# Projection ahead of attention: first sums by tile, transfers and maxima moved

## The chip, the cores and the metric

The kernel runs on one core of a Trainium2 chip. The metric is the device time of one execution in microseconds, the median of several. PE is the tensor engine (PEld its weight loads), DVE the vector engine, ACT the scalar engine, POOL GpSimd, SP the engine that here only issues transfers.

## The reference, cut to what matters

A block of a transformer on 2 x 2048 tokens of 512 channels: a mixture of experts, attention, the mixture of experts again, each behind a layer norm without scale or bias:

```
x = x + 0.5 * ffn(layernorm(x));  x = x + attn(layernorm(x));  x = x + 0.5 * ffn(layernorm(x))
attn: q = x @ Wq + bq  (16 heads of 32)    k = x @ Wk + bk, v = x @ Wv + bv  (one head of 32)
      out = softmax(q k^T / sqrt(32)) v @ Wo + bo
```

The change lies in the projection, which makes q, k and v of `layernorm(x)` and stores `x + bo`.

## The kernel before, in words

Stages follow each other with a barrier between them: `route` and `experts`, then `project` and the rest of `attention`, then `route`, `experts` and `combine`. Each engine runs its own instructions in the order in which they are written, and waits at semaphores (`wait_ge`). The order is written out by hand; there is no planner.

`project` (from line 1094) takes the 4096 tokens as 32 tiles of 128, and four tiles as a turn (`TURN`, eight turns, `NTURN`). The experts left x in two tensors in memory that have to be added. For turns 0 and 1 (`ADDED`) both are loaded (`got`, `other`, line 1184 and 1186) and DVE adds them tile by tile (`add_sums`, 1366). For the later turns SP loads one, and POOL issues a transfer that adds the second to it (`bring`, 1242), which waits for the load first. Four turns are loaded at once (`LEAD`), the others as the loop of SP comes to them. `got` has six buffers.

The work on tile t is spread over slots, and in slot s every engine does what is due of several tiles:

- DVE `moments` of tile s-1 (1374 to 1381: mean and variance), after `add_sums` of tile s in the first eight slots;
- POOL `deviation` of tile s-1 (1228, 1231: one over the square root, and the shift), after `output_bias` of tile s-4 (1237: adds `bo` to x);
- ACT `normalise` of tile s-2 (1324) and `high` of tile s-3 (1331: the part of the transposed tile that goes to PE in reduced precision);
- PE `transposes` of tile s-3 (1263), DVE `low` of tile s-4 (1388: the rest);
- PE `keys` (K and V, twelve matmuls, lines 1268 to 1270) at the first slot of a turn from slot 8 on, `queries` (twelve matmuls for one of four groups of heads) in every slot from 8 to 39, and `values` (1288, small transposes) in the third slot of a turn;
- one slot later ACT and DVE take the results: `queries` (ACT 1336 the high part `qhi`, DVE 1394 the low part `qlo`), `keys` (ACT 1342 to 1347, DVE 1400), `values` (DVE 1404). SP stores both parts of a query (`store_q`, 1195 and 1197), and ACT overwrites a part only when the store of a turn ago has landed (`s_q`).

In the last 16 slots (`FIRST` = 24) the stage also does 64 blocks of row maxima of scores ahead for the first group of attention (`first_maxima`): PE makes a block of 128 x 512 scores in one of two banks of PSUM, `pF` (1298), and DVE reduces it (1408). PE waits until the reduction of two blocks earlier is done. Each of these slots has four (`SOME`): two ahead of all other work of the slot, two behind it, on PE and on DVE. Their queries are read back from memory by SP after turn 3 (`ahead["queries"]`, 12 transfers, line 1452).

`FIRST`, `SOME` and the slot offsets stand at the top of the function; `SLOTS` is 41. `first_blocks(s, half)` gives the block numbers of half a slot.

Of the kernel before, what the change touches and what calls it, by code (L numbers as in the profile page):

```python
# [23 lines left out]
TURN = 4  # L24
# [11 lines left out]
A = 32  # L36


def begin(eng, *sems):
    for s in sems:  # L40
        eng.sem_inc(s, A)  # L41
# [1052 lines left out]
def project(nc, tag, k, prep, q_d, kT, v_sb, sums, xb_d, ahead):  # L1094
# [17 lines left out]
    with ExitStack() as ctx:  # L1112
# [16 lines left out]
        pV = m.ps("pV", [P, TURN, DH])  # L1129
        pF = m.ps("pF", [P, 2, 512])  # L1130
        s_g = m.sems("g", RING)
        s_on = m.sems("on", RING)
        s_xo = m.sems("xo", RING)
        s_add = m.sem("add")
# [23 lines left out]

        def loads(i):

            return i // RING + (2 if i % RING < ADDED else 1)

        def brought(i):
            return i // RING + (0 if i % RING < ADDED else 1)

        def first_blocks(s, half):

            n = SOME * (s - FIRST) + SOME // 2 * half
            return range(n, n + SOME // 2) if 0 <= n < ahead["items"] else ()

        def comes(t):
            return 0 <= t < NT
# [4 lines left out]
        with nc.Block() as block:  # L1177
            @block.sync
            def _(sp):
                begin(sp, *s_q, *s_g, *s_xo)  # L1180

                def load(i):
                    sp.wait_ge(s_xo[i % RING], A + i // RING * 16)
                    sp.dma_start(got[i % RING][:, :, :], turn_view[0][i, :, :, :]).then_inc(s_g[i % RING], 16)
                    if i < ADDED:
                        sp.dma_start(other[i][:, :, :], turn_view[1][i, :, :, :]).then_inc(s_g[i % RING], 16)

                def store_x(i):
                    sp.wait_ge(s_xb, A + (i + 1) * TURN)
                    dst = xb_d[i * (TURN * P):(i + 1) * (TURN * P), :].rearrange("(t p) c -> p t c", p=P)  # L1190
                    sp.dma_start(dst, got[i % RING][:, :, :]).then_inc(s_xo[i % RING], 16)

                def store_q(c, g):
                    sp.wait_ge(s_hi, A + c * GPC + (g + 1))
                    sp.dma_start(q_view[c, g, 0, :, :], qhi[g].bitcast(F32)).then_inc(s_q[g], 16)
                    sp.wait_ge(s_lo, A + c * GPC + (g + 1))
                    sp.dma_start(q_view[c, g, 1, :, :], qlo[g].bitcast(F32)).then_inc(s_q[g], 16)

                for i in range(LEAD):
                    load(i)  # L1200
                for i in range(NTURN + 1):
                    if i + LEAD < NTURN:
                        load(i + LEAD)
                    for g in range(GPC):

                        if g == 2 and i < NTURN:
                            store_x(i)
                        if i > 0:
                            store_q(i - 1, g)
                    if i == 3:  # L1210
                        for g in range(GPC):
                            sp.wait_ge(s_q[g], A + 32)
                        ahead["queries"](sp)
                for b in range(RING):
                    sp.wait_ge(s_xo[b], A + 16 * len(range(b, NTURN, RING)))
                for g in range(GPC):
                    sp.wait_ge(s_q[g], A + 32 * CHUNKS)

            @block.gpsimd
            def _(pool):  # L1220
                begin(pool, s_rd, s_rs, s_xb)

                def deviation(t, j):
                    pool.wait_ge(s_ve, A + t + 1)
                    pool.sem_inc(k["pool_on"], 1)
                    pool.wait_ge(s_xn, A + t - TURN + 1)
                    pool.sem_inc(k["pool_on"], 1)
                    pool.tensor_tensor(rstd[:, j:j + 1], ve[:, j:j + 1], k["half"][:, 0:1], ALU.pow).then_inc(s_rd, 1)
                    pool.wait_ge(s_rd, A + t + 1)
                    pool.sem_inc(k["pool_on"], 1)  # L1230
                    pool.tensor_scalar(shift[:, j:j + 1], mv[:, j, 0:1], rstd[:, j:j + 1], -1.0, ALU.mult, ALU.mult
                                       ).then_inc(s_rs, 1)

                def output_bias(t):
                    pool.wait_ge(s_xn, A + t + 1)
                    pool.sem_inc(k["pool_on"], 1)
                    pool.tensor_tensor(x_tile(t), x_tile(t), bo_sb[:, :], ALU.add).then_inc(s_xb, 1)

                def bring(i):
                    pool.wait_ge(s_g[i % RING], A + 16 * loads(i))  # L1240
                    pool.sem_inc(k["pool_on"], 1)
                    pool.dma_start(got[i % RING][:, :, :], turn_view[1][i, :, :, :], accum_op=ALU.add
                                   ).then_inc(s_on[i % RING], 16)

                for s in range(SLOTS):

                    i = (s + 6) // TURN
                    if (s + 6) % TURN == 0 and ADDED <= i < NTURN:
                        bring(i)
                    if comes(s - BIAS):  # L1250
                        output_bias(s - BIAS)
                    if comes(s - 1):
                        deviation(s - 1, (s - 1) % TURN)

            @block.tensor
            def _(pe):
# [6 lines left out]
                        ins = pe.transpose(pT[:, j % 2, c, :], xn[:, j, c * P:(c + 1) * P], k["ident"][:, :])  # L1263
                    ins.then_inc(s_tr, 1)

                def products(out, high, low, b):
                    for c in range(CK):
                        pe.matmul(out, high[:, c, :], xh[b][:, c, :], start=c == 0, stop=False)
                        pe.matmul(out, high[:, c, :], xl[b][:, c, :], start=False, stop=False)
                        ins = pe.matmul(out, low[:, c, :], xh[b][:, c, :], start=False, stop=c == CK - 1)  # L1270
                    return ins

                def queries(i, g, b):
                    pe.wait_ge(s_lo, A + i * GPC + (g - 1))
                    own = slice(g * P, (g + 1) * P)
                    products(pQ[:, g % 2, :], wqh[:, :, own], wql[:, :, own], b).then_inc(s_pq, 1)

                def keys(i, b):
                    pe.wait_ge(s_xl, A + (i + 1) * TURN)
# [11 lines left out]
                def first_maxima(n):  # L1291
                    unit, part = n // (S // 512), n % (S // 512)
                    t, h = unit // HG, unit % HG
                    if n == 0:
                        pe.wait_ge(ahead["in"], A + 48)
                        pe.wait_ge(s_kl, A + CHUNKS // 2)
                    pe.wait_ge(ahead["reduced"], A + n - 1)
                    pe.matmul(pF[:, n % 2, :], ahead["q"][0:3 * DH, h, t * P:(t + 1) * P],
                              kT[0:3 * DH, part * 512:(part + 1) * 512], start=True, stop=True
                              ).then_inc(ahead["made"], 1)  # L1300

                for s in range(SLOTS):
                    for n in first_blocks(s, 0):
                        first_maxima(n)
                    if comes(s - TRANS):
                        transposes(s - TRANS, (s - TRANS) % TURN)
                    if comes(s - PROD):
                        i, j = (s - PROD) // TURN, (s - PROD) % TURN
                        if j == 0:
                            keys(i, i % 2)  # L1310
                        queries(i, j, i % 2)
                        if j == 2:
                            values(i)
                    for n in first_blocks(s, 1):
                        first_maxima(n)

            @block.scalar
            def _(act):
# [42 lines left out]
            def _(dve):  # L1361
                begin(dve, s_add, s_st, s_ve, s_vb, s_xl, s_lo, s_kl, ahead["reduced"])

                def add_sums(t, i, j):
                    dve.wait_ge(s_g[i % RING], A + 16 * loads(i))
                    dve.tensor_tensor(x_tile(t), x_tile(t), other[i][:, j, :], ALU.add).then_inc(s_add, 1)

                def moments(t, i, j):
# [39 lines left out]
                    dve.tensor_reduce(ahead["mx"][:, n:n + 1], pF[:, n % 2, :], X, ALU.max).then_inc(ahead["reduced"], 1)  # L1408

                for s in range(SLOTS):  # L1410
                    for n in first_blocks(s, 0):
                        first_maxima(n)
                    if comes(s - SPLIT):
                        low(s - SPLIT, (s - SPLIT) // TURN, (s - SPLIT) % TURN)
                    if s < ADDED * TURN:
                        add_sums(s, s // TURN, s % TURN)
                    if comes(s - 1):
                        moments(s - 1, (s - 1) // TURN, (s - 1) % TURN)
                    if comes(s - PARTS):
                        i, j = (s - PARTS) // TURN, (s - PARTS) % TURN  # L1420
                        queries(i, j)
                        if j == 1:
                            keys(i)
                        if j == 3:
                            values(i)
                    for n in first_blocks(s, 1):
                        first_maxima(n)
                dve.wait_ge(ahead["reduced"], A + ahead["items"])
                dve.wait_ge(s_kl, A + NTURN)
# [650 lines left out]
```

## Time and profile before

| | us |
|---|---|
| median of 3 runs without a profile | 3122.11 (3119.02 to 3122.38) |
| the profiled execution, own time | 3151.85 |
| its span, first to last instruction | 3150.1 |
| projection, from its first transfer to the next stage's first work on DVE | 616.6 to 816.4 |
| PE busy in the whole span | 2751.5 (87%) |
| DVE, POOL, ACT busy | 2045.3, 2243.3, 1523.3 |

The page gives busy time per engine. A busy share of PE is no distance from the end: what counts is which engine the others wait for in a stretch. The views used below are the stretches (busy time of each engine between two times), the waits (who waited for whom) and the timeline (instructions in order of time). The mean granted clock of PE is 0.931 of full speed over the span; it is 0.50 from 616 to 650 us and 1.00 from 660 to 816.

### The profile page before, as it was taken

The page shows a single profiled execution, that of the slowest core. Times are in us where ns is not written, and L with a number is a line of the kernel's source. Part 1 is how long each engine was busy: PE and PEld are TensorE (multiplying, and loading weights), DVE is VectorE, ACT ScalarE, POOL GpSimd, SP SyncE. Part 2 cuts the span into 40 slices and gives each one's busy share as a digit, 9 for nine tenths or more (in the row PEclk, how much of TensorE's full clock was granted, in tenths as well). Part 3 has the DMA queues.
Part 4 walks back from the last instruction along what each step waited for, and adds up shares of the span by engine and source line. Part 5 has one row for each costly group of instructions (what it writes and reads, how often), then busy time and mean ns, then how long its engine had stood idle before and what let it go on. Part 6 is the DMA issues. An engine that isn't in the chain of part 4 may idle for free. (4 is left out here: it accounts for less than half of the span.)

```text
span 3150.1 us, 44567 instructions
## 1 busy us (share of the span) xinstructions
PE 2751.5 (87%) x15016; PEld 1648.4 (52%) x15016; DVE 2045.3 (65%) x3954; ACT 1523.3 (48%) x2871; POOL 2243.3 (71%) x1461
## 2 busy tenths in 40 slices
PE   7967777489899999999999999999999776888870
PEld 4644444266555555555555555555554474555540
DVE  7843222257788888788788887887874494333334
ACT  5622222153476666566566665765656451222220
POOL 2248888563399979799798897997989323778770
PEclk9979888689999999999999999999999767999995
DMA  5579999895388888799797887987877454999998
GB/s 209 212 208 247 236 237 240 182 287 193 84 183 180 170 179 177 153 194 181 165 184 159 188 166 157 194 173 174 175 149 165 139 211 136 221 234 241 234 183 325
DMA packets 221450, 608.27 MB, mean 193 GB/s; under 512 B 34476, under 2 KB 35500, under 8 KB 193320
## 3 DMA queue, kind: packets, MB, share of 16 engines
q0 software_dynamic: 91760, 376.49, 59.2%
q1 hardware_dynamic: 125240, 220.55, 21.3%
q10 hardware_dynamic: 4224, 8.39, 0.7%
q8 instruction: 121, 1.98, 0.3%
q14 instruction: 105, 0.86, 0.1%
HBM read 230.94 MB, written 155.24 MB: 123 GB/s over the span
## 5 line engine op out<-in xcount | busy, mean ns | idle before, releaser
L1924 DVE TENSOR_REDUCE attention_mx<-attention_pM 128x1 f32<-128x512 f32 x1984 | 1209.3, 682 | 185.1 <-PE attention_pM L1808 184.3
L1755 ACT ACTIVATE attention_prob<-attention_pS 128x512 f32<-128x512 f32 x2048 | 1032.7, 627 | 566.4 <-PE attention_pS L1787 561.7
L1692 POOL TENSOR_TENSOR attention_pair<-attention_prob 128x1024 f32<-128x1024 f32 x380 | 989.8, 2768 | 108.5 <-ACT attention_prob L1755 105.1
L1787 PE MATMUL attention_pS<-attention_qT,prep_kT 128*128 128x512 f32 x2048 | 841.3, 413 | 4.7 <-ACT attention_prob L1755 3.8
L1808 PE MATMUL attention_pM<-prep_kT,attention_qT 96*128 96x512 f32 x1984 | 787.8, 398 | 0.8
L1787 PEld LDWEIGHTS attention_pS<-attention_qT,prep_kT 128*128 128x128 f32 x2048 | 387.3, 189 | 313.0 <-issue 210.2
L768 POOL DMA_INDIRECT sum<-experts_res,c_table x256 | 403.5, 1576 | 124.3 <-issue 82.3
L1836 PE MATMUL attention_pO<-attention_prob,attention_v 128*32 128x512 f32 x4096 | 491.7, 598 | 0.0
L1808 PEld LDWEIGHTS attention_pM<-prep_kT,attention_qT 96*128 96x128 f32 x1984 | 377.9, 190 | 89.3 <-DVE attention_mx L1924 14.4
L752 POOL DMA_INDIRECT experts_rows<-xn_rows,c_table x256 | 250.1, 977 | 104.1 <-issue 74.9
L797 PE MATMUL experts_pT<-c_ident,experts_rows 128*128 128x128 f32 x1024 | 169.8, 307 | 117.1 <-issue 68.0
L943 DVE TENSOR_SCALAR experts_res<-experts_pD,experts_rows 128x512 f32<-128x512 f32 x128 | 93.5, 749 | 271.0 <-DMA sum<-experts_res,c_table 170.4
L1836 PEld LDWEIGHTS attention_pO<-attention_prob,attention_v 128*32 128x32 f32 x4096 | 110.1, 109 | 252.7 <-issue 147.6
L1692 POOL TENSOR_TENSOR prep_acc<-attention_prob 128x1024 f32<-128x1024 f32 x68 | 167.0, 2493 | 86.6 <-ACT attention_prob L1755 83.7
L797 PEld LDWEIGHTS experts_pT<-c_ident,experts_rows 128*128 128x128 f32 x1024 | 141.5, 209 | 152.5 <-issue 121.6
L922 DVE COPY experts_xT<-experts_pT 128x512 f32<-128x512 f32 x128 | 88.3, 690 | 204.5 <-PE experts_pT L797 143.7
L892 ACT ACTIVATE experts_res<-experts_pD,experts_rows 128x512 f32<-128x512 f32 x128 | 85.3, 686 | 250.4 <-DMA sum<-experts_res,c_table 180.0
L309 POOL TENSOR_TENSOR route_eqp<-route_eq,route_count 128x1536 f32<-128x1536 bf16 (+1 forms) x16 | 48.4, 3024 | 201.9 <-ACT route_count L429 201.9
L1692 POOL TENSOR_TENSOR attention_acc<-attention_prob 128x1024 f32<-128x1024 f32 x64 | 158.8, 2541 | 5.6 <-ACT attention_prob L1755 2.2
L884 ACT ACTIVATE experts_sg<-experts_pU 128x256 f32<-128x256 f32 x80 | 30.7, 383 | 265.6 <-PE experts_pU L814 121.2
L878 ACT ACTIVATE experts_xT<-experts_pT 128x512 f32<-128x512 f32 x128 | 76.4, 597 | 115.1 <-PE experts_pT L797 59.4
L814 PE MATMUL experts_pU<-experts_xT,experts_wup 128*64 128x256 f32 x1024 | 126.1, 402 | 1.6 <-DVE experts_xT L922 1.6
(184 smaller groups left out, 3195.3 us busy)
## 6 DMA issues: line engine op xcount, KB each, us to landing
prep_acc<-attention_pair POOLq DMA_DIRECT2D x96, 1024.0 KB, 8.1
attention_acc<-attention_pair POOLq DMA_DIRECT2D x90, 1024.0 KB, 7.7
attention_qT<-q_parts SPq DMA_DIRECT2D x96, 256.0 KB
xn_rows<-route_xn SPq DMA_DIRECT2D x16, 1152.0 KB, 6.6
experts_wup<-in_L_ffn_w_up_dram SPq DMA_DIRECT2D x64, 256.0 KB
q_parts<-prep_acc SPq DMA_DIRECT2D x64, 256.0 KB, 4.3
prep_acc<-prep_acc POOLq DMA_DIRECT2D x16, 1024.0 KB, 7.5
ahead_wup<-in_L_ffn_w_up_dram SPq DMA_DIRECT2D x64, 256.0 KB, 9.1
```

What stands on the lines that cost most here:

```text
L752: pool.indirect_dma_start(rows[e % RING][:, a * HALVES + h, :], None, xn_d, bass.IndirectOffsetOnAxis(ap=k["table"][:, 2 * e + a, h:h + 1] ...
L768: pool.indirect_dma_start(sums[a], bass.IndirectOffsetOnAxis(ap=k["table"][:, 2 * e + a, h:h + 1], axis=0), res[e % 2][:, a, h, :], None, ...
L797: t = pe.transpose(pT[:, half, o:o + P], rows[e % RING][:, a * HALVES + h, c:C:CK], k["ident"][:, :])
L814: t = pe.matmul(pU[n % 2][a * H:(a + 1) * H, v, :], wts[b][0][:, a, c, v * H:(v + 1) * H], xT[e % 2][:, c, a, :], start=c == 0, stop=c == ...
L922: dve.tensor_copy(xT[e % 2][:, 2:4, a, :], pT[:, 1, :].rearrange("p (c n) -> p c n", c=2)).then_inc(s_cd, 1)
L943: dve.tensor_scalar(res[e % 2][:, 1, h, :], pD[:, h, 1, :], rows[e % RING][:, HALVES + h, C + 2 * e + 1:C + 2 * e + 2], None, ALU.mult).th ...
L1692: pool.tensor_tensor(to[:, part], prob[2 * n % PROBS][:, part], prob[(2 * n + 1) % PROBS][:, part], ALU.add).then_inc(s_pair, 1)
L1755: act.activation(prob[t % PROBS][:, h * QT:(h + 1) * QT], pS[:, at, :], ACT.Exp).then_inc(s_ex, 1)
L1787: pe.matmul(pS[:, n % 3, :], kT[:, key:key + P], qT[g][:, h, :], start=True, stop=True).then_inc(s_sc, 1)
L1808: pe.matmul(pM[:, r % RING, :], qT[g][0:3 * DH, h, t * P:(t + 1) * P], kT[0:3 * DH, key:key + 512], start=True, stop=True).then_inc(s_mp, 1)
L1836: ins = pe.matmul(pO[h * DH:(h + 1) * DH, :], v_sb[:, batch * STEPS + t, :], prob[t % PROBS][:, h * QT:(h + 1) * QT], start=t == 0, stop=t ...
L1924: dve.tensor_reduce(mx[:, unit, part:part + 1], pM[:, r % RING, :], X, ALU.max).then_inc(s_mr, 1)
```

## The change

Five edits, all in `project`:

1. The first turn is loaded tile by tile: eight transfers (two tensors, four tiles) in the place of two, each pair with a semaphore of its own (`s_first`), for which `add_sums` waits in turn 0.
2. `bring(i)` is issued in slot 4i - 4 in the place of 4i - 6.
3. POOL does `deviation` ahead of `output_bias`.
4. DVE does `moments` of the tile before ahead of `add_sums`.
5. The four maxima of a slot stand on PE among the products of that slot's query, one ahead of each three matmuls, and on DVE all four behind the slot's other work.

```
-            return i // RING + (2 if i % RING < ADDED else 1)
+            return i // RING + (2 if 0 < i % RING < ADDED else 1 if i % RING else 0)      # loads(i)
...
-        def first_blocks(s, half):
-            n = SOME * (s - FIRST) + SOME // 2 * half
-            return range(n, n + SOME // 2) if 0 <= n < ahead["items"] else ()
+        def first_blocks(s):
+            n = SOME * (s - FIRST)
+            return tuple(range(n, n + SOME)) if 0 <= n < ahead["items"] else ()
...
SP
-                for i in range(LEAD):
+                for j in range(TURN):
+                    for part, to in ((0, got[0]), (1, other[0])):
+                        sp.dma_start(to[:, j, :], turn_view[part][0, :, j, :]).then_inc(s_first[j], 16)
+                for i in range(1, LEAD):
                     load(i)
...
POOL
-                    i = (s + 6) // TURN
-                    if (s + 6) % TURN == 0 and ADDED <= i < NTURN:
+                    i = (s + 4) // TURN
+                    if (s + 4) % TURN == 0 and ADDED <= i < NTURN:
                         bring(i)
+                    if comes(s - 1):
+                        deviation(s - 1, (s - 1) % TURN)
                     if comes(s - BIAS):
                         output_bias(s - BIAS)
-                    if comes(s - 1):
-                        deviation(s - 1, (s - 1) % TURN)
...
PE
-                def products(out, high, low, b):
+                def products(out, high, low, b, blocks=()):
                     for c in range(CK):
+                        if blocks:
+                            first_maxima(blocks[c])
...
                 for s in range(SLOTS):
-                    for n in first_blocks(s, 0):
-                        first_maxima(n)
...
-                        queries(i, j, i % 2)
+                        queries(i, j, i % 2, first_blocks(s))
...
-                    for n in first_blocks(s, 1):
-                        first_maxima(n)
...
DVE
                 def add_sums(t, i, j):
-                    dve.wait_ge(s_g[i % RING], A + 16 * loads(i))
+                    if i == 0:
+                        dve.wait_ge(s_first[j], A + 32)
+                    else:
+                        dve.wait_ge(s_g[i % RING], A + 16 * loads(i))
...
                 for s in range(SLOTS):
-                    for n in first_blocks(s, 0):
-                        first_maxima(n)
                     if comes(s - SPLIT):
                         low(s - SPLIT, (s - SPLIT) // TURN, (s - SPLIT) % TURN)
+                    if comes(s - 1):
+                        moments(s - 1, (s - 1) // TURN, (s - 1) % TURN)
                     if s < ADDED * TURN:
                         add_sums(s, s // TURN, s % TURN)
-                    if comes(s - 1):
-                        moments(s - 1, (s - 1) // TURN, (s - 1) % TURN)
...
-                    for n in first_blocks(s, 1):
+                    for n in first_blocks(s):
                         first_maxima(n)
```

## Rows read from the trace of the kernel before

**Rows 1.** Stretches: bounds, length, busy us (count) of five engines, PEclk, DMA share, GB/s
```profile
625.00:630.00 5.00, 0.36 (x2) 0.36 (x3) 4.46 (x11) 0.81 (x1) 1.03 (x2) 0.50 1.05 391
...
680.00:700.00 20.00, 20.00 (x101) 16.20 (x100) 11.06 (x25) 10.94 (x18) 12.21 (x16) 1.00 1.08 314
...
741.00:766.00 25.00, 22.39 (x100) 16.05 (x99) 20.37 (x39) 10.05 (x16) 8.42 (x12) 1.00 0.35 131
```

**Rows 2.** Waits of PE from 616 to 790 us: total, times, longest
```profile
PE attentionp_pF L1298 <- DVE attention_mx L1408: 6.6, 12, 0.6
```

**Rows 3.** Timeline, the head: start, duration, engine, line, operation
```profile
616.62 0.38 SPq L1184 DMA_DIRECT2D attentionp_got<-sum  x1
...
624.47 1.29 DVE L1366 TENSOR_TENSOR attentionp_got<-attentionp_got,attentionp_other 128x512 f32<-128x512 f32 x2 [29.84 <-DMA attentionp_other<-sum]
...
633.17 1.37 POOL L1242 DMA_DIRECT2D attentionp_got<-sum  x1 [4.44 <-DMA attentionp_got<-sum]
...
635.36 0.27 POOL L1231 TENSOR_SCALAR attentionp_shift<-attentionp_mv,attentionp_rstd 128x1 f32<-128x1 f32 x1 [0.21 <-POOL attentionp_rstd L1228]
...
635.66 0.81 ACT L1324 ACTIVATE attentionp_xn<-attentionp_got,attentionp_shift,attentionp_rstd 128x512 f32<-128x512 f32 x1 [6.08 <-POOL attentionp_shift L1231]
...
636.57 1.27 POOL L1237 TENSOR_TENSOR attentionp_got<-attentionp_got,prep_bo 128x512 f32<-128x512 f32 x1
...
636.99 0.69 DVE L1388 TENSOR_TENSOR attentionp_xl<-attentionp_pT,attentionp_xh 128x512 fp32r<-128x512 f32 x1 [6.57 <-ACT attentionp_xh L1331]
...
647.66 0.81 ACT L1324 ACTIVATE attentionp_xn<-attentionp_got,attentionp_shift,attentionp_rstd 128x512 f32<-128x512 f32 x1 [2.69 <-POOL attentionp_shift L1231]
...
649.29 0.78 PE L1268 MATMUL attentionp_pK<-attentionp_xh,prep_wkvh 128*128 128x512 f32 x1
```

**Rows 4.** Timeline, PE: first maxima, products of the keys in two turns
```profile
715.25 0.63 PE L1298 MATMUL attentionp_pF<-prep_kT,attention_qT 96*128 96x512 f32 x2
...
716.87 0.39 PE L1268 MATMUL attentionp_pK<-attentionp_xh,prep_wkvh 128*128 128x512 f32 x1
...
741.67 0.40 PE L1268 MATMUL attentionp_pK<-attentionp_xh,prep_wkvh 128*128 128x512 f32 x1
...
742.37 0.40 PE L1268 MATMUL attentionp_pK<-attentionp_xh,prep_wkvh 128*128 128x512 f32 x1
```

**Rows 5.** Timeline, PE: maxima and transposes around the end of slot 24
```profile
721.77 0.63 PE L1298 MATMUL attentionp_pF<-prep_kT,attention_qT 96*128 96x512 f32 x2
...
722.95 1.10 PE L1298 MATMUL attentionp_pF<-prep_kT,attention_qT 96*128 96x512 f32 x2 [0.55 <-DVE attention_mx L1408]
...
723.88 0.60 PE L1263 MATMUL attentionp_pT<-c_ident,attentionp_xn 128*128 128x128 f32 x4
...
727.12 0.63 PE L1298 MATMUL attentionp_pF<-prep_kT,attention_qT 96*128 96x512 f32 x2
```

**Rows 6.** Timeline, DVE in slots 26 and 27
```profile
732.58 0.68 DVE L1400 TENSOR_TENSOR prep_kT<-attentionp_k,prep_kT 32x512 fp32r<-32x512 f32 x1
...
736.09 0.69 DVE L1388 TENSOR_TENSOR attentionp_xl<-attentionp_pT,attentionp_xh 128x512 fp32r<-128x512 f32 x1
...
737.86 0.75 DVE L1394 SCALAR_TENSOR_TENSOR prep_acc<-attentionp_pQ,prep_bqs,prep_acc 128x512 fp32r<-128x512 f32 x1
...
738.85 2.57 DVE L1408 TENSOR_REDUCE attention_mx<-attentionp_pF 128x1 f32<-128x512 f32 x4 [0.24 <-PE attentionp_pF L1298]
```

**Rows 7.** Timeline, ACT in slot 25
```profile
725.52 0.69 ACT L1336 ACTIVATE prep_acc<-attentionp_pQ,prep_bqs 128x512 fp32r<-128x512 f32 x1 [4.26 <-DMA q_parts<-prep_acc]
```

**Rows 8.** Timeline, the end of the stage
```profile
810.53 0.63 PE L1298 MATMUL attentionp_pF<-prep_kT,attention_qT 96*128 96x512 f32 x2
...
810.97 1.29 DVE L1408 TENSOR_REDUCE attention_mx<-attentionp_pF 128x1 f32<-128x512 f32 x2 [1.56 <-PE attentionp_pF L1298]
...
812.18 0.74 DVE L1394 SCALAR_TENSOR_TENSOR prep_acc<-attentionp_pQ,prep_bqs,prep_acc 128x512 fp32r<-128x512 f32 x1
```

**Rows 9.** The line of the queries' low stores, its last line
```profile
DMA to landing us min/median/max: 2.0/3.3/14.1
```

More of the change, by code:

```diff
@@ L1131, in project @@
         s_g = m.sems("g", RING)
+        s_first = m.sems("first", TURN)
         s_on = m.sems("on", RING)
@@ L1179, in _ @@
             def _(sp):
-                begin(sp, *s_q, *s_g, *s_xo)
+                begin(sp, *s_q, *s_g, *s_first, *s_xo)
                 def load(i):
@@ L1271, in products, with queries @@
                     return ins
-                def queries(i, g, b):
+                def queries(i, g, b, blocks):
                     pe.wait_ge(s_lo, A + i * GPC + (g - 1))
                     own = slice(g * P, (g + 1) * P)
-                    products(pQ[:, g % 2, :], wqh[:, :, own], wql[:, :, own], b).then_inc(s_pq, 1)
+                    products(pQ[:, g % 2, :], wqh[:, :, own], wql[:, :, own], b, blocks).then_inc(s_pq, 1)
                 def keys(i, b):
```

## The prediction, made before the changed kernel ran

> **What bounds the kernel now.** I read the stretches first. All edits lie in `project`, from 616.6 us (its first transfer) to 816.4 us. It has three phases. Until 649.29 PE waits for the first keys. Then PE is busy without a gap: 20.00 of 20.00 us in the second row of [rows 1]. From slot 24 on (715.25, [rows 4]) it is busy 22.39 of 25.00 us, the third row, and the waits say for whom it stops: the next maximum's matmul waits for a reduction of DVE [rows 2]. So PE's order of work is the path in the last two phases, and in the first whatever brings tile 5 to PE, since `keys(0)` stands behind the transposes of tile 5.
>
> **The head now.** I read it next, in order of time. The DMAs bring 391 GB/s [rows 1]; two turns' tensors of 1.05 MB each land for the first sum at 624.47. POOL then stands at `bring(2)` (slot 2) until turn 2's load is there at 633.17: 4.44 us idle, and the deviations of tiles 1 and 2, whose moments were ready, come after it: shift of tile 1 at 635.36 + 0.27 = 635.63. Tile 5 is normalised at 647.66 and the first product of the keys starts at 649.29, so 1.63 us from one to the other [rows 3].
>
> **The change, part by part.** A slot ends, at E, where PE's last matmul of it lets the next one start.
>
> *Transfers two slots later, deviation ahead of the bias.* POOL now has the deviations of tiles 0, 1 and 2 ahead of `bring(2)`, which stands in slot 4 and still waits for 633.17. I take its issue at today's price, so that the shift made behind it is again done at 635.63, but it is tile 3's and not tile 1's. The row at 635.66 (normalise) leads to the low part at 636.99 [rows 3]; in the new order this low part is tile 2's, and tile 5's moments follow it. Low part and moments take 737.86 - 736.09 = 1.77 [rows 6], so they are ready at 638.76. POOL meanwhile does bias 0 (1.27), deviation 4 (0.94, from 635.63 to 636.57), bias 1 and deviation 5: 635.63 + 1.27 + 0.94 + 1.27 + 0.94 = 640.05 [rows 3], later than the moments, so POOL sets it. Plus 1.63 and the sequencers' steps: the keys start at about 641.8. That is 7.5 us sooner. Of these, bias ahead of deviation (the old order) would cost one 1.27 back. Every later `bring(i)` has five slots instead of seven until its turn's moments. Slots before 24 take some 4 us of PE, so some 20 us are left, while the slowest landing in this stage is 14.1 us [rows 9]; no stall there. Bounds for this part: 3 (the wait turns up at tile 3 and costs two more slots) to 9.
>
> *First sums by tile.* Eight transfers of 0.26 MB in the place of two of 1.05 MB. From 616.62 to 624.47 are 7.85 us, of which 2.10 MB at 391 GB/s take 5.4, so 2.5 is latency; the first pair of 0.52 MB should land 2.5 + 1.3 = 3.8 us after the first issue, at about 620.4, four sooner. But these four us are hidden: with the first sum at 624.5 the moments of tile 3 would be ready about 632.7, still before `bring(2)` is through. I take 0 to 0.5 and count nothing. SP has six more issues and four more semaphores to start; an issue takes 0.38 [rows 3], 2.3 us in all, beside transfers that already queue. If they delayed turn 2's load, all of that delay would stand on the path: 0 to 2, I take 0.
>
> The row says that the stream runs at 391 GB/s with transfers of 1 MB. The Trainium skill (DMA: Bandwidth & Descriptors, Anatomy of one DMA, and Bandwidth) counts about 2.0 us fixed per DMA beside its bytes and says to batch to 1 MiB or more. By that, if the fixed parts stood one behind the other, six more would cost about 12 us (an estimate) in front of turn 2, more than the head gains.
>
> *Moments ahead of the next sum.* DVE's sum (about 0.6 of pitch) leaves the way of tile 5's moments; they wait for POOL anyway by 638.76 against the 639.1 at which POOL turns to them, so 0 to 0.6, and I count nothing beyond the 7.5. What is late next are POOL's biases.
>
> *Maxima among products.* 64 maxima in slots 24 to 39, four in each. Today the four stand together around a slot's end: 721.77 to 723.88 [rows 5] is 2.11 us, where four matmuls at a pitch of 0.233 (0.70 for three, [rows 4]) would be 0.93; 1.18 is waiting on pF, which has two banks. Transposes and twelve products take 723.88 to 727.12, 3.24. Slot without keys: 5.35. Turn of four slots: 741.67 - 716.87 = 24.80 [rows 4].
>
> New, each maximum stands ahead of three products, 0.93 apart, while a reduction takes 0.69. That would hide all, but DVE now has all four reductions behind its low part, moments and query. Its last reduction starts 0.44 behind its matmul ([rows 8], 810.53 and 810.97) with a pitch of 0.64 (2.57 for four, [rows 6]), so DVE turns to the next slot at E - 0.93 + 0.44 + 0.64 = E + 0.15. Low part, moments and query: 738.6 - 736.09, about 2.5. First reduction done at E + 3.3. The third maximum needs it and could start at E + 2.3 (slot 3.24 + 0.93 = 4.17, less the 1.87 of eight matmuls behind it). So PE stops for 1.1 us inside a query, and the slot takes 3.4 + 1.87 = 5.27. The wait moves and stays. What differs are the other slots: with keys 3.24 + 2.80 + 0.93 = 6.97, no stall (today 8.16: the turn of 24.80 less the other three); in the slot in which DVE also does the keys' low part (0.70, 732.58, [rows 6]) 5.97, plus 0.36 of values' transposes; in the one after it 4.90, since DVE has caught up 0.36. Turn: 6.97 + 5.27 + 6.33 + 4.90 = 23.47.
>
> Turns 4 and 5: 23.47 each. Turn 6 has no moments after its first slot; there the query's part waits for ACT's (PE's end + 0.2 + 0.69): 6.97 + 4.23 + 5.29 + 3.87 = 20.36. Turn 7, without transposes: 6.53 + 4.23 + 5.29 + 3.87 = 19.92. Sum 87.2, against 810.53 - 715.25 = 95.3 now: 8.1 less.
>
> One stall comes back. In slot 25 ACT's query part waits until 725.52 for a store of queries, 3.75 after E at 721.77 [rows 5, 7]. Today two reductions run ahead of it and PE loses nothing. Now all four stand behind it: ACT at E + 3.3 (the slot before ends 0.45 later against the stores), DVE's query until E + 4.7, first reduction E + 5.4, slot 7.3 in the place of 5.27: 2.0 back. Bounds 0 to 3. After the last product DVE has no two reductions ahead of the last query part: it ends at E + 1.65, today 812.92 - 810.53 = 2.39 [rows 8]: 0.7 less on the way to the last store.
>
> **Sum.** 7.5 + 8.1 - 2.0 + 0.7 = 14.3 us. The profiled execution took 3151.85 (span 3150.1); it would take 3137.6. The median of the runs timed without a profile is 3122.11, 29.7 lower; all parts are durations on chip, so I take off the same 14.3: 3107.8.
>
> **Rivals.**
> 1. *Only the head gains.* If DVE's chain in a slot is longer than I add up (the stalled slots would need 0.7 more, 12 of them without keys), the maxima give nothing: 7.5 to 8, 3114.5. For it: the stalled slot comes out at 5.27 against 5.35, a tie in three of four slots of a turn. Against: the slots with keys and the last two turns have room on DVE.
> 2. *The small transfers slow the stream.* A 256 KB transfer needs at least 2.0 us from issue to landing [rows 9]. If the eight went one after the other, 16 us stand where 7.1 are now, turn 2's load is about 9 late and the head loses 1.5 instead of gaining 7.5: sum 5.3, 3116.8. Against: the second transfer is issued 0.4 us after the first, and queued ones overlap at 391 GB/s. The page's rule named above points this way and further.
> 3. *Head stalls again*: `bring(2)` stays in front of tile 3, and its wait or turn 2's accumulation holds tile 8's moments; head gains 3, sum 9.8: 3112.3.
> 4. *The other side: stores hold DVE in every slot.* The wait of slot 25 repeats. With all reductions behind the query part, each of the 11 other slots without keys would take 7.3 instead of about 5.2, some 22 us in all: 14.3 - 22 = -8, 3130. It decides where a query's store lands later than four slots (21 us) after its issue. Against: the slowest landing is 14.1 [rows 9], and of ACT's 32 waits one is on a store.
> 5. *No part reaches the end*, 3122.1: only if PE's order were not the path. Against it are 20.00 of 20.00 and the 10% idle in [rows 1, 2].
>
> **How the numbers follow.** Forecast (12 to 17 less) 0.54; rival 1 0.15; rival 2 0.06; rival 3 0.11; rival 4 0.05; rival 5 0.04; more than 17 less 0.05. No change means within 0.2%, 6.2 us, about what a measurement of this kernel can tell. Faster: the forecast, more, rivals 1 and 3 nearly whole, a third of 2: 0.85. Same 0.10, slower 0.05. The range reaches from 16.5 less (3105.6, less 2 for the spread of the medians, 3103) to rivals 3 and 1 and their edge, 3116.
>
> **What would show it.** Right: first sum near 620.5; `bring(2)` behind tile 2's shift, still idle until 633; the first product of the keys near 641.8; K to K in turns 4 to 5 near 23.5; in slots without keys one PE wait of about 1 us, on the third maximum, and none on the fourth; a longer one in slot 25. Wrong: turn 2's load later than 634; PE waiting for tiles in slots 9 to 12; a wait of `moments` on an accumulation; slots without keys of 5.5 or more; the keys starting before 640 or after 644.

## The result, and the profile after

| | us |
|---|---|
| median before / after, 22 runs each | 3124.06 / 3119.19 |
| ratio, 95% interval | 0.9985, 0.9978 to 0.9991 |
| profiled execution after, its span | 3123.33, 3121.6 |
| predicted | 3107.8 (3103 to 3116) |

The change takes 4.9 us off, where 14.3 were predicted: the direction was right, the size a third, the time outside the range. The two profiled executions are 28 us apart, but 11 of these lie ahead of the projection, which starts at 606.00 in the one and 616.62 in the other, and the change touches nothing there. So from here all times called "of the stage" count from the projection's first transfer:

| us of the stage | before | after | predicted |
|---|---|---|---|
| first sum | 7.85 | 3.40 | 3.8 |
| `bring(2)` issued, turn 2's load is there | 16.55 | 17.83 | 16.55 |
| first product of the keys | 32.67 | 26.80 | 25.2 |
| last maximum | 193.91 | 191.21 | 179.4 |
| next stage's first work on DVE | 199.81 | 197.35 | 185.5 |

(The forecast puts the end of the last product at 180.3; in the new order the last maximum stands 0.93 ahead of it, in the old one right behind it.)

The timeline of the kernel after, the head (columns as in [rows 3]):

```profile
606.00 0.33 SPq L1202 DMA_DIRECT2D attentionp_got<-sum  x1
...
609.40 0.69 DVE L1371 TENSOR_TENSOR attentionp_got<-attentionp_got,attentionp_other 128x512 f32<-128x512 f32 x1 [26.22 <-DMA attentionp_other<-sum]
...
623.83 1.37 POOL L1246 DMA_DIRECT2D attentionp_got<-sum  x1 [6.21 <-DMA attentionp_got<-sum]
...
631.16 0.81 ACT L1326 ACTIVATE attentionp_xn<-attentionp_got,attentionp_shift,attentionp_rstd 128x512 f32<-128x512 f32 x1 [1.36 <-POOL attentionp_shift L1235]
...
632.80 0.78 PE L1274 MATMUL attentionp_pK<-attentionp_xh,prep_wkvh 128*128 128x512 f32 x1
```

The head gained what its mechanism promised: tile 5 is normalised and 1.64 us later the keys start, 5.9 us sooner than before; 1.3 of the missing 1.6 are turn 2's load. Then slot 25, the timeline of PE, ACT and DVE (to set against [rows 5, 7]):

```profile
706.69 0.48 PE L1304 MATMUL attentionp_pF<-prep_kT,attention_qT 96*128 96x512 f32 x1
707.71 0.40 PE L1304 MATMUL attentionp_pF<-prep_kT,attention_qT 96*128 96x512 f32 x1
...
716.20 0.69 ACT L1338 ACTIVATE prep_acc<-attentionp_pQ,prep_bqs 128x512 fp32r<-128x512 f32 x1 [11.30 <-DMA q_parts<-prep_acc]
716.92 0.75 DVE L1399 SCALAR_TENSOR_TENSOR prep_acc<-attentionp_pQ,prep_bqs,prep_acc 128x512 fp32r<-128x512 f32 x1 [8.65 <-ACT prep_acc L1338]
...
718.32 0.80 PE L1304 MATMUL attentionp_pF<-prep_kT,attention_qT 96*128 96x512 f32 x1 [9.52 <-DVE attention_mx L1413]
...
718.91 0.63 PE L1274 MATMUL attentionp_pQ<-attentionp_xh,prep_wqh 128*128 128x512 f32 x1
```

A bracket says how long the engine was idle and for whom. Read upward from PE: its third maximum of the slot waits 9.52 us for a reduction of DVE, DVE stands 8.65 for ACT's high part, and ACT stands 11.30 for a store of a turn ago. ACT's wait was 4.26 before [rows 7] and cost PE 0.55. The waits of PE from 606 to 800 us have it in one line (total, times, longest), as [rows 2] does before:

```profile
PE attentionp_pF L1304 <- DVE attention_mx L1413: 15.2, 8, 9.5
```

The turns of four slots can be read from the first product of the keys in slots 24, 28 and 32, as in [rows 4]:

```profile
699.73 0.48 PE L1274 MATMUL attentionp_pK<-attentionp_xh,prep_wkvh 128*128 128x512 f32 x1
...
733.17 0.48 PE L1274 MATMUL attentionp_pK<-attentionp_xh,prep_wkvh 128*128 128x512 f32 x1
...
757.60 0.48 PE L1274 MATMUL attentionp_pK<-attentionp_xh,prep_wkvh 128*128 128x512 f32 x1
```

Turn 4 takes 33.44 (forecast 23.47 + 2.0), turn 5 takes 24.43 (23.47). Last, three stretches of the kernel after (columns as in [rows 1]): two ahead of the store's landing, one behind the stop.

```profile
686.00:701.00 15.00, 15.00 (x77) 12.09 (x76) 9.15 (x20) 8.56 (x14) 10.01 (x13) 1.00 1.08 254
701.00:716.00 15.00, 7.81 (x36) 6.03 (x34) 6.07 (x13) 3.04 (x5) 4.10 (x6) 0.88 1.08 259
718.00:722.00 4.00, 3.68 (x9) 2.80 (x10) 2.69 (x5) 0.07 (x1) 0.00 (x0) 0.50 1.05 407
```

The DMA engines are full (1.08) up to the landing. After the stop PE's clock is granted at half (0.50, that is 1.2 GHz): a matmul takes 0.63 in the place of 0.40.

### The profile page after: what moved, and what is told of

Read it like the earlier page. It is cut to its first block and busy times, and to the rows that moved or that the text cites. A ratio compares the mean times of both kernels' runs of the same rounds, so it can differ in the third digit from the quotient of the medians.

```text
span 3121.6 us, 44593 instructions
## 1 busy us (share of the span) xinstructions
PE 2737.5 (88%) x15016; PEld 1643.7 (53%) x15016; DVE 2045.3 (66%) x3954; ACT 1521.8 (49%) x2871; POOL 2241.9 (72%) x1461
## 3 DMA queue, kind: packets, MB, share of 16 engines
q1 hardware_dynamic: 125336, 220.55, 21.5%
## 5 line engine op out<-in xcount | busy, mean ns | idle before, releaser
L1811 PEld LDWEIGHTS attention_pM<-prep_kT,attention_qT 96*128 96x128 f32 x1984 | 378.1, 191 | 88.2 <-DVE attention_mx L1927 13.7
L1839 PEld LDWEIGHTS attention_pO<-attention_prob,attention_v 128*32 128x32 f32 x4096 | 110.2, 109 | 252.5 <-issue 147.7
```

The costliest lines, as they stand in the source:

```text
L1811: pe.matmul(pM[:, r % RING, :], qT[g][0:3 * DH, h, t * P:(t + 1) * P], kT[0:3 * DH, key:key + 512], start=True, stop=True).then_inc(s_mp, 1)
L1839: ins = pe.matmul(pO[h * DH:(h + 1) * DH, :], v_sb[:, batch * STEPS + t, :], prob[t % PROBS][:, h * QT:(h + 1) * QT], start=t == 0, stop=t ...
```

## The experiments

The theory, called A where a name is needed: the head's gain is given back in slot 25, because turn 3's first stores land when the DMA queues have worked off what was put into them, and not when PE is done; with all reductions behind the query part, every microsecond that PE comes sooner is one more of waiting. The rivals: the new order on PE and DVE is slower by itself; the small loads or the later adding transfers cost what the order gains. In the table, "landing" is the end of ACT's wait for the store, and "stop" PE's longest stop in slot 25; ratios are to the kernel before on the same chip.

| kernel | ratio, 95% interval | keys | landing | stop | last maximum |
|---|---|---|---|---|---|
| before | | 32.67 | 108.9 | 0.55 | 193.91 |
| after | 0.9985, 0.9978 to 0.9991 | 26.80 | 110.2 | 9.52 | 191.21 |
| head_only | 1.0005, 0.9996 to 1.0014 | 26.92 | 110.4 | 2.97 | 196.33 |
| maxima_only | 0.9977, 0.9968 to 0.9986 | 32.81 | 110.7 | 3.93 | 190.99 |
| read_late | 0.9952, 0.9938 to 0.9966 | 27.16 | no wait | 0.77 | 180.23 |
| bring_split | 0.9967, 0.9955 to 0.9979 | 28.03 | 107.1 | 5.25 | 188.17 |
| before_read | 0.9999, 0.9991 to 1.0008 | 32.96 | no wait | 0.56 | 194.61 |
| head_read | 0.9983, 0.9974 to 0.9991 | 27.77 | no wait | 0.56 | 190.91 |
| two_ahead | 0.9932, 0.9920 to 0.9944 | 26.52 | no wait | 0.31 | 175.84 |
| first_whole | 0.9946, 0.9934 to 0.9958 | 26.38 | no wait | 0.80 | 179.28 |
| lead5 | 0.9982, 0.9973 to 0.9991 | 26.89 | 109.4 | 9.61 | 189.66 |
| best | 0.9926, 0.9913 to 0.9940 | 26.44 | no wait | 0.28 | 174.80 |
| read_half | 0.9952, 0.9941 to 0.9964 | 26.92 | no wait | 0.80 | 181.89 |
| bring7_old | 0.9985, 0.9974 to 0.9996 | 27.02 | 110.6 | 6.01 | 190.93 |

**head_only** and **maxima_only** take the change apart: the one is edits 1 to 4 with the maxima as before, the other edit 5 alone.

```
head_only      for n in first_blocks(s, 0): first_maxima(n)    # ahead of the slot's work, PE and DVE
               ...
               for n in first_blocks(s, 1): first_maxima(n)    # behind it
maxima_only    products(out, high, low, b, blocks): first_maxima(blocks[c]) ahead of each three
```

> The edits of the head alone (first sums by tile, transfers two slots later, deviation ahead of bias, moments ahead of the sum); maxima stand in pairs as before. Theory A (the transfers are saturated until slot 25, so the store for which ACT waits there lands about 108.5 us after the stage's first transfer whatever the head does): the keys start 7.5 us sooner, ACT's wait in slot 25 grows from 4.3 to about 11, PE stands before the third maximum behind slot 25 for some 6 us, and the stage is only 0 to 2 us shorter than before. Theory B (the stall comes from the reductions' new place alone): the stage is about 7 us shorter.

> The edit of the maxima alone, head as before. Theory A: ACT's wait in slot 25 ends at the same 108.9 us after the stage's start as before and is about 4 us long; PE stops about 3 us in that slot; the maxima phase gains about 5 to 6 and the end 0.7, so the stage is 5 to 6 us shorter: as fast as the whole change or a little faster. Theory B (new place of the reductions makes the long stall by itself): a stall of 9 us here too, stage 3 us longer than before.

The head alone starts the keys 5.75 us sooner and gives nothing at the end (1.0005). The maxima alone give 7 us. Together they give 5. In head_only slot 25 is not the only place that takes the gain. Its first maximum, which stands at the very start of slot 24 there, already waits 1.74 us for the reads of queries made ahead; matmuls then run at 0.63, and the stop of 2.97 in slot 25 follows. Timeline of head_only, PE:

```profile
702.06 0.73 PE L1302 MATMUL attentionp_pF<-prep_kT,attention_qT 96*128 96x512 f32 x2 [1.74 <-DMA attention_qT<-q_parts]
...
704.47 0.63 PE L1272 MATMUL attentionp_pK<-attentionp_xh,prep_wkvh 128*128 128x512 f32 x1
```

ACT's waits in slot 25, in the timelines of head_only and then of maxima_only:

```profile
717.04 0.69 ACT L1340 ACTIVATE prep_acc<-attentionp_pQ,prep_bqs 128x512 fp32r<-128x512 f32 x1 [7.34 <-DMA q_parts<-prep_acc]
```

```profile
713.46 0.69 ACT L1334 ACTIVATE prep_acc<-attentionp_pQ,prep_bqs 128x512 fp32r<-128x512 f32 x1 [5.71 <-DMA q_parts<-prep_acc]
```

Counted from each stage's start (606.62 and 602.75) they end at 110.4 and 110.7: the same, though PE is 6 us further in the one. The landing does not follow PE.

**read_late** takes load from the DMA queues in front of these stores: of the 12 reads of queries that SP issues after turn 3, only the first three stay there, and three follow after each of the next turns.

```
-        def first_queries(sp):
-            begin(sp, *s_q)
-            for g in range(GPC):
-                load(sp, 0, g)
+        def first_queries(sp, g):
+            if g == 0: begin(sp, *s_q)
+            load(sp, 0, g)
...
-                    if i == 3: ahead["queries"](sp)
+                    if 3 <= i < 3 + GPC: ahead["queries"](sp, i - 3)
```

> The changed kernel, but the queries of groups 1 to 3 are read back one group after each of turns 4 to 6, where all four were read after turn 3: 2.4 MB less stand in front of the stores of turn 3. Theory A: at some 300 GB/s they take 7 to 8 us out of the way of the stores; ACT's wait in slot 25 falls from 11.3 to 4 or less, PE's stop there from 9.5 to at most 3, no slow clock behind it; stage 7 to 9 us shorter than in the changed kernel. Theory C (the later bring of turn 7 alone is in the way): at most 2 us shorter.

The wait is gone. The median is 13.7 us below the kernel before's on the same chip (15 by the ratio), the stage is 13.5 shorter than before, and PE stops for 0.77 in slot 25 and 1.64 in slot 26. Timeline of read_late, PE, the third maximum of slots 25 and 26, and the keys' first products of slots 28 and 32:

```profile
712.30 0.50 PE L1305 MATMUL attentionp_pF<-prep_kT,attention_qT 96*128 96x512 f32 x1 [0.77 <-DVE attention_mx L1414]
...
718.38 0.50 PE L1305 MATMUL attentionp_pF<-prep_kT,attention_qT 96*128 96x512 f32 x1 [1.64 <-DVE attention_mx L1414]
...
726.08 0.48 PE L1275 MATMUL attentionp_pK<-attentionp_xh,prep_wkvh 128*128 128x512 f32 x1
...
749.75 0.48 PE L1275 MATMUL attentionp_pK<-attentionp_xh,prep_wkvh 128*128 128x512 f32 x1
```

Turn 5 is 23.67, where the prediction added up 23.47.

**bring_split** issues `bring(2)` as the change does and the later adding transfers as before.

```
-                    i = (s + 4) // TURN
-                    if (s + 4) % TURN == 0 and ADDED <= i < NTURN:
+                    if s == 4: bring(ADDED)
+                    i = (s + 6) // TURN
+                    if (s + 6) % TURN == 0 and ADDED < i < NTURN:
                         bring(i)
```

> The changed kernel with only the first adding transfer two slots later and those of turns 3 to 7 in their old slots. Theory C (turn 7's adding transfer, issued 4 us before the stores of turn 3 wait, is what holds them): ACT's wait in slot 25 falls back towards 4, stage 5 or more shorter. Theory A (a backlog of all transfers since the stage's start): the same bytes stand in front of the stores; wait in slot 25 within 2 us of 11.3, stage within 2 us of the changed kernel.

The landing comes 3.1 us sooner and the stage ends 3.05 sooner, more than A as written allowed (2 us): when the adding transfers go counts as well. The stretch of 15 us that answers to the first of after moves 291 GB/s instead of 254, at the same share of the engines. Stretch and timeline of bring_split:

```profile
684.10:699.10 15.00, 15.00 (x77) 12.07 (x76) 9.31 (x21) 8.34 (x14) 9.97 (x13) 1.00 1.07 291
```

```profile
711.17 0.69 ACT L1340 ACTIVATE prep_acc<-attentionp_pQ,prep_bqs 128x512 fp32r<-128x512 f32 x1 [7.06 <-DMA q_parts<-prep_acc]
```

**before_read** and **head_read** put the edit of read_late on the kernel before and on head_only.

> The kernel before with only the queries of groups 1 to 3 read back later. If the transfers matter only through PE's stop in slot 25, which the kernel before does not have, nothing changes: within 2 us of before, ACT's wait in slot 25 gone. If the reads' mere presence slowed PE or DVE elsewhere, it would be 3 us or more faster.

> The edits of the head with the later reads, maxima in pairs as before. Theory A: with the backlog out of the way the head's 5.9 us reach the end: stage 5 to 7 us shorter than before, where the head alone gave nothing. If the head were worth nothing in itself (lost at any later point), it stays within 2 us of before.

Both came as expected. Later reads alone change nothing (0.9999), because PE lost nothing to the wait before; the head alone changes nothing; the two together give 5 us by the medians (0.9983), 3.0 in the profiled stage, where PE still waits 1.02 in slot 24 for the first of the reads. So the head's gain was real and waits on transfers took it, and it is no merit of the later reads by themselves. With the maxima as well the gain is 14 to 15.

**two_ahead** is read_late with DVE's first two reductions of a slot ahead of its query part, the order on PE unchanged:

```
+                    for n in first_blocks(s)[:2]:
+                        first_maxima(n)
                     if comes(s - PARTS):
...
-                    for n in first_blocks(s):
+                    for n in first_blocks(s)[2:]:
                         first_maxima(n)
```

> The changed kernel with the later reads, and on DVE the first two of a slot's four reductions ahead of the query's low part, the other two behind it. Theory: in slots without keys PE's third maximum waits for the first reduction, which stands behind low part, moments and query (2.5 us); with the query's 0.75 out of the way the slot is set by DVE's own work, 5.1 in the place of 5.24, and slots with DVE's keys part lose their long wait of 1.64: turn 23.4 to 21.5 or 22; about 4 us in all. Rival: DVE's total is the bound already and the order on it changes nothing (within 1 us).

The stop of about a microsecond per slot, which the prediction said would stay, is for the most part a matter of DVE's order: here it is 0.31 in slot 25 and 0.37 in slot 26, and PE's stops in turn 4 add up to 1.77 in the place of 2.82. The turn takes 22.8, where 21.5 to 22 were expected. The last maximum comes 4.4 us sooner than in read_late, 3.8 when counted from the first product of the keys. Timeline of two_ahead, PE:

```profile
710.71 0.50 PE L1305 MATMUL attentionp_pF<-prep_kT,attention_qT 96*128 96x512 f32 x1 [0.31 <-DVE attention_mx L1414]
...
715.50 0.50 PE L1305 MATMUL attentionp_pF<-prep_kT,attention_qT 96*128 96x512 f32 x1 [0.37 <-DVE attention_mx L1414]
```

**first_whole** is read_late without edit 1 (the first turn in two transfers again); **bias_first** is read_late without edit 3, **sum_first** without edit 4.

```
first_whole    for i in range(LEAD): load(i)                  # SP; add_sums waits for s_g in turn 0 too
bias_first     output_bias(s - BIAS); deviation(s - 1, ...)   # POOL
sum_first      add_sums(s, ...); moments(s - 1, ...)          # DVE
```

> The changed kernel with the later reads, but the first turn loaded in two transfers as before. Prediction's claim (the four us of the earlier first sum are hidden behind the adding transfer's wait): the keys start at the same time or, since turn 2's load landed 1.3 us later in the changed kernel, up to 1.3 us sooner. If the sums by tile carry the head: 2 us or more later.

> The changed kernel with the later reads, and on POOL the bias ahead of the deviation as before. By the prediction's chain the keys start 1.3 to 2.6 us later than the 27.2 us of the same kernel with the deviation first. Rival: POOL has the time, no difference.

> The changed kernel with the later reads, and on DVE the sum ahead of the moments as before. By the prediction POOL's chain covers it: the keys start 0 to 0.6 us later than 27.2. Rival: DVE's chain sets the pace of the slots (each two slots pass once through the sum): 1.2 us or more later.

Without edit 1 turn 2's load is there at 16.96 instead of 18.19, the keys start 0.8 sooner and the last maximum comes 0.95 sooner: the first sum, 4.7 us earlier with edit 1, is hidden, and the small transfers cost a microsecond. (In this profile POOL's 1.42 us ahead of `bring(2)` are put down to DVE, but `bring` waits for nothing but its load.) The same shows over all profiles: with small transfers `bring(2)` starts at 17.5 to 18.8 (eleven kernels), without them at 16.6 to 17.0 (five). The bias ahead of the deviation costs 1.5 at the keys (28.64), the sum ahead of the moments 0.3 (27.43). Their times are one execution each, 3112.2 and 3108.0, beside a median of 3124.7 for the kernel before on that chip, and tell no more than that.

**lead5** changes the size `LEAD` from 4 to 5: a fifth turn is loaded at the start, so that 1 MB moves into a stretch in which the DMAs idle, and out of the one before the stores.

> The changed kernel with five turns loaded at the start in the place of four, so that turn 5's load also stands in the queue at once; the reads of the queries as in the changed kernel. Theory A (transfers are saturated from 35 to 110 us of the stage, and only 25 to 30 us, share 0.34, is idle): the idle stretch takes some 1 MB of what now stands behind it, so the store for which ACT waits lands 2 to 3.5 us sooner, and PE's stop of 9.5 falls by as much or by half as much again; stage 2 to 4 us shorter than in the changed kernel. If the wait is made by the reads or the last adding transfer alone, not by all bytes since the start: no difference.

Stretches of after and then of lead5, some 25 to 30 us into the stage:

```profile
631.00:636.00 5.00, 3.97 (x12) 3.30 (x13) 4.09 (x10) 2.59 (x4) 4.79 (x7) 0.50 0.34 63
```

```profile
630.72:635.72 5.00, 3.88 (x13) 3.27 (x14) 4.01 (x9) 2.59 (x4) 4.79 (x7) 0.58 0.99 206
```

The gap is filled (0.99 of the engines in the place of 0.34), the landing comes 0.8 sooner and the stop stays, 9.61. I had expected 2 to 4 us. The form of A in which all bytes since the start of the stage are one backlog falls; what holds the stores seems to be put into the queues late.

**read_half** leaves six of the 12 reads after turn 3 and issues the other six after turn 4. **bring7_old** is the kernel after with only the last adding transfer, `bring(7)`, in its old slot 22.

```
read_half      if 3 <= i < 5: for g in (2*i - 6, 2*i - 5): ahead["queries"](sp, g)
bring7_old     bring(7) at s == 22, the others at (s + 4) % TURN == 0
```

> The changed kernel with groups 0 and 1 read back after turn 3 and groups 2 and 3 after turn 4: half of the reads ahead of the stores. If the reads' bytes in the queue set where the store lands, its wait falls by about half of what all three later groups took away: the store lands some 5 us sooner (105 in the place of 110.2), PE's stop of 9.5 becomes 4 to 5, stage some 5 us shorter. Rival: it is the reads' start that blocks the queue of issues, so half of them hold the store as long.

> The changed kernel with only the last adding transfer (turn 7) in its old slot 22, those of turns 2 to 6 in the new ones. If it is the one that overlaps the reads and the stores of turn 3 which cost 3 us of the wait, the store lands near 107 as with turns 3 to 7 in their old slots. Rival: it is the earlier ones (the idle stretch of transfers from 25 to 30 us that turn 3's transfer fills there), and it stays at 109 to 110.

read_half came out by neither of its two forecasts. Half of the reads away does not halve the stop, it removes ACT's wait altogether (stop 0.80, 0.9952, as good as read_late). bring7_old came out by its rival: `bring(7)` alone does not bring back the 3 us of bring_split, the landing stays at 110.6. The stop is shorter (6.01) only because PE had already stood 1.71 us before its first maximum in slot 24 and then made some matmuls at 0.63; turn 4 is as long as in the kernel after (33.43 and 33.44). This chip ran every kernel some 26 us slower, so only the ratios are compared.

bring7_old also answers, in part, a rival that no run was made for: that the store is late because SP, which issues in order, stands in the reads' issue and comes to it late. Timeline of bring7_old, SP and ACT (its stage starts at 614.79):

```profile
698.14 13.08 SPq L1457 DMA_DIRECT2D attention_qT<-q_parts  x12
711.26 0.53 SPq L1196 DMA_DIRECT2D q_parts<-prep_acc  x1
...
725.39 0.69 ACT L1340 ACTIVATE prep_acc<-attentionp_pQ,prep_bqs 128x512 fp32r<-128x512 f32 x1 [11.28 <-DMA q_parts<-prep_acc]
```

Here the store is issued at 96.5 of the stage, 4.4 us later than in the kernel after (92.05), and lands only 0.4 later (110.6 and 110.2). So the moment of issue did not set the landing in these two.

**best** is two_ahead with first_whole:

> Later reads, two reductions ahead of the query's low part, and the first turn loaded in two transfers: 0.8 to 1 us less than with the sums by tile, so 21 to 23 us below the kernel before. If the two edits were not additive: as with the two reductions ahead alone, 20 us.

3102.73 against 3124.7 of the kernel before: 22 us less, 17 less than the change as given. The last maximum comes at 174.80.

## Why the prediction was wrong, step by step

- *The path and its phases*: right. Each edit that moved PE's order moved the end, once slot 25 let it through.
- *Head, 7.5*: 5.9 measured. The mechanism holds: POOL stands at `bring(2)` behind three deviations, and the keys start 1.64 after tile 5's normalising (1.63 forecast). The term taken as 0 (bounds 0 to 2) for six more issues in front of turn 2's load was 1.3; first_whole shows that 1.2 of it comes from edit 1. The fixed cost of about 2 us per DMA that the Trainium skill gives (DMA: Bandwidth & Descriptors, Anatomy of one DMA) is stated for DMAs issued by GpSimd, and these are SP's; it points the right way, but the 12 us of fixed parts one behind the other did not come here: six more queued transfers cost 1.3 us together. Rival 2 falls with it.
- *The small terms of the head*: right. The first sum came at 3.40 (3.8) and is hidden. The sum ahead of the moments costs 0.3 (0 to 0.6), the bias ahead of the deviation 1.5 (1.27).
- *Maxima, 8.1*: right in its mechanism, 7.0 in size. read_late shows it without the wait of slot 25: the four slots of turn 4 take 6.98, 5.23, 6.54 and 4.92 (6.97, 5.27, 6.33 and 4.90), turns 6 and 7 some 0.3 more each than forecast (20.36 and 19.92). From the start of slot 24 to the end of the last product read_late takes 88.3 (87.2), before takes 95.3. Turn 5 of the kernel after was 1.0 longer than forecast; in its slot 30 PE waited 1.64 and ran on at a granted clock of 0.65 (749 to 752 us), which the same wait did not bring in read_late.
- *The end, 0.7*: 5.21 against 5.90 from the last product to the next stage, 0.7.
- *The store wait of slot 25, 2.0 back, bounds 0 to 3*: this is the step that failed. It priced the new order behind the wait, but took the wait itself over from the trace of before, as if the store's landing came as much sooner as PE, and even shortened it by 0.45 (ACT free "at E + 3.3"). The landing stood at 108.9 before and 110.2 after. ACT was ready 5.7 us sooner, so its wait was 11.30 and PE lost 9.52 in one piece (3.1 forecast), with a few matmuls at half clock behind it. Turn 4 is 8.0 longer than forecast and 9.8 longer than in read_late (23.66), where the wait is gone: the term of 2.0 should have been 9.8. Rival 4 had this mechanism, DVE held by stores, but in every slot and under the condition that landings take over 20 us; it came in one slot, at a landing of under 18.

The bookkeeping of the stage in the two profiles: 14.3, less 1.6 of the head, 8.0 of turn 4, 1.0 of turn 5, 0.6 of turns 6 and 7, and some 0.6 in the slots before 24, leaves 2.5, which is what the stage shows (199.81 to 197.35). The medians say 4.9 (2.8 to 6.9); the rest is not explained.

What warned in the profile: I had looked for the slowest landing (14.1, [rows 9]) and compared it with the 20 us until its buffer is needed. Two things are wrong with that. The 14.1 is the slowest of one line, the queries' low stores, and not of the stage: in the kernel after the adding transfers land 9.7 to 15.9 us after their issue. And it is a distance measured from the issue of the store, while the issue itself is queued. In the kernel after, SP's own row of the timeline shows it; the last line is that of the low stores' landings, as [rows 9] before:

```profile
698.05 0.43 SPq L1196 DMA_DIRECT2D q_parts<-prep_acc  x1
698.53 0.43 SPq L1198 DMA_DIRECT2D q_parts<-prep_acc  x1
...
699.95 4.51 SPq L1192 DMA_DIRECT2D x_rows<-attentionp_got  x1
704.50 7.31 SPq L1196 DMA_DIRECT2D q_parts<-prep_acc  x1
...
DMA to landing us min/median/max: 2.0/6.7/17.9
```

The 12 reads, issued from 82.9 to 92.0 of the stage, come first. Both parts of the store were ready at 84.9, and SP comes to them at 92.05, at 698.05 and 698.53 of the span. ACT goes on at 716.20, when both have landed, some 18 us later for 256 KB each; two of the transfers behind them take 4.51 and 7.31 us to issue alone. Before, the same store was ready at 90.1 and issued at 94.2: PE's lead of more than 5 us had shrunk to 2.2 at the issue, and the landing took 3.5 longer. The stretch before had said the same in [rows 1]: a DMA share of 1.08 from 680 to 700.

Shown: waits on transfers take the head's gain (head_only, before_read, head_read), and the reads made ahead cause the one in slot 25 (read_late, read_half). Open: how half of the reads can remove the whole of it, since taking reads away changes both the bytes in the queue and the moment at which SP comes to the store; why the same share of the DMA engines moves 254 to 259 GB/s in the 30 us before the landing, where before it moved 309 and 305 (the stretches from 80 us of the stage), and which of the adding transfers of turns 3 to 6 gives bring_split its 3 us; bring7_old only rules out the last one alone.

## What to carry to other kernels

Where the DMA engines are full, take a landing as a date on their clock and not as a distance from the engine that waits (five kernels here landed this store at 109.4 to 110.7 of the stage, while ACT was ready for it anywhere from 98.0 to 105.0): work that comes sooner may only wait longer, so price every wait on a transfer again from its absolute time. Before crediting a faster head or a new order, find the next transfer that the path has to meet and ask what is queued in front of it. Reads that are only fetched ahead belong behind the stores that a buffer waits for.

## What the hardware did that I had not expected

- A store of 256 KB took up to 17.9 us from issue to landing, at a DMA share of 1.08; the same line's fastest took 2.0.
- SP's issue of one transfer, 0.33 us at the start of the stage, took up to 7.31 us with full queues.
- The same share of the DMA engines (1.07 to 1.08) moved between 254 and 309 GB/s.
- After a stop of 9.52 us PE was granted half the clock for some microseconds; after the stop of 1.74 in head_only its clock was 0.62 over the next 4 us. After stops of 0.55 to 0.8 it stayed at 1.00, and after stops of 1.64 it was 0.65 once and 1.00 in read_late.
